# A low-rank adapter kernel: the first sixteen tiles loaded in halves by two DMA queues, and stored four at a time

## The reference

```python
x: (64 sequences, 64 tokens, 1024) f32      ids: (64,) int32, values 3 to 7
A: (8 adapters, 1024, 16) f32               B: (8 adapters, 16, 1024) f32

B_sel, A_sel = B[ids], A[ids]
Bx  = einsum('bni,bri->bnr', x, B_sel)
out = x + einsum('bnr,bor->bno', Bx, A_sel) * 1.0
```

## Time and profile before

| | us |
|---|---|
| median of 3 runs | 92.23 (92.19 to 92.32) |
| the profiled execution | 91.81 |
| its span, first to last instruction | 90.0 |

### The profile page before, as it was taken

One profiled execution on the slowest core, in us unless ns is written; L12 is line 12 of the kernel. 1 busy time (PEld: TensorE's weight loads), 2 busy tenths in 40 slices (PEclk: granted clock), 3 DMA queues, 4 the chain that ended last, 5 costly groups with the idle time before them and its releaser, 6 DMA issues.

```text
span 90.0 us, 3579 instructions
## 1 busy us (share of the span) xinstructions
PE 80.6 (90%) x1451; PEld 60.7 (67%) x1451; DVE 59.7 (66%) x111; ACT 59.4 (66%) x154; POOL 62.9 (70%) x141
## 2 busy tenths in 40 slices
PE   3995999999999999999999999998999999989300
PEld 3974778768787878787777868685778686633100
DVE  0309968277777786859595959595939595999100
ACT  1429869959696969695959686877595868524200
POOL 6103992999999999979696979696859692900000
PEclk9999999999999999999999999999999999999975
DMA  1999999999999999999999999999999999997990
GB/s 29 325 412 422 410 408 408 402 415 413 399 409 404 410 409 400 400 415 413 419 422 413 417 419 410 415 426 406 419 417 415 417 413 400 404 391 306 408 395 36
DMA packets 9249, 34.82 MB, mean 387 GB/s; under 512 B 402, under 2 KB 914, under 8 KB 9234
## 3 DMA queue, kind: packets, MB, share of 16 engines
q1 hardware_dynamic: 7520, 27.79, 77.2%
q10 hardware_dynamic: 1714, 6.82, 18.8%
HBM read 17.83 MB, written 16.78 MB: 384 GB/s over the span
## 4 chain that ended last, share of the span: by engine, by line
PE 83%; DMA 6%; ACT 4%; issue 1%
PE t_bank L255 35%; PE bx_bank L268 21%; PE y_banks L288 18%; DMA x_all<-in_A 6%; PE y_banks L315 2%; PE t_bank L319 2%; ACT x_all L365 1%; PE bx_bank L319 1%; PE y_banks L242 1%; ACT b_table L369 1%; PE bx_bank L315 1%; ACT x_all L424 1%; ACT x_t L377 1%; PE t_bank L315 1%; PE bx_bank L242 0%
## 5 line engine op out<-in xcount | busy, mean ns | idle before, releaser
L465 DVE TENSOR_TENSOR x_all<-y_banks,x_all 128x1024 f32<-128x1024 f32 x29 | 35.5, 1224 | 15.5 <-PE y_banks L288 15.1
L377 ACT COPY x_t<-t_bank 128x512 f32<-128x512 f32 x64 | 34.4, 590 | 13.7 <-PE t_bank L255 12.8
L198 POOL CAST a_duo<-a_table 128x512 fp32r x64 | 36.6, 615 | 3.7 <-PE y_banks L288 2.1
L255 PE MATMUL t_bank<-ident,x_all 128*128 128x128 f32 x256 | 35.0, 280 | 1.2 <-DMA x_all<-in_x 0.8
L255 PEld LDWEIGHTS t_bank<-ident,x_all 128*128 128x128 f32 x256 | 27.4, 141 | 8.4 <-issue 5.2
L188 POOL COPY b_duo<-b_table 128x256 f32 x64 | 22.9, 401 | 5.8 <-PE bx_bank L268 5.8
L268 PE MATMUL bx_bank<-x_t,b_duo 128*32 128x64 f32 x1024 | 20.8, 222 | 0.0
L268 PEld LDWEIGHTS bx_bank<-x_t,b_duo 128*32 128x32 f32 x1024 | 15.7, 109 | 5.5 <-issue 5.5
L288 PE MATMUL y_banks<-a_duo,bx_parts 64*128 64x512 f32 x112 | 17.3, 421 | 0.3 <-issue 0.3
L456 DVE TENSOR_TENSOR bx_parts<-bx_bank,bx_parts 32x64 fp32r<-32x64 f32 x64 | 14.1, 220 | 1.5 <-ACT bx_parts L392 0.4
L392 ACT CAST bx_parts<-bx_bank 32x64 fp32r<-32x64 f32 x64 | 13.0, 204 | 1.9 <-PE bx_bank L268 1.3
(11 more groups left out here) (31 smaller groups left out, 21.2 us busy)
## 6 DMA issues: line engine op xcount, KB each, us to landing
x_all<-in_x SPq DMA_DIRECT2D x3, 3072.0 KB, 30.7
out_y<-x_all ACTq DMA_DIRECT2D x2, 3072.0 KB, 17.8
x_all<-in_x SPq DMA_DIRECT2D x3, 1024.0 KB, 12.4
out_y<-x_all SPq DMA_DIRECT2D x1, 3072.0 KB, 14.5
out_y<-x_all SPq DMA_DIRECT2D x6, 512.0 KB, 4.7
x_all<-in_x SPq DMA_DIRECT2D x4, 512.0 KB, 7.2
x_all<-in_x SPq DMA_DIRECT2D x1, 2048.0 KB, 20.0
out_y<-x_all SPq DMA_DIRECT2D x1, 2048.0 KB, 10.4
```

Of the source, the lines that this page charges most:

```text
L198: last = nc.gpsimd.tensor_copy(a_duo[duo % 2][:, k, :], a_table[:, bass.ds(adapters[k] * BANK, BANK)])
L255: last = nc.tensor.transpose(t_bank[unit % 2][:, c * P:(c + 1) * P], x_all[:, 2 * duo + tile, at:at + P], ident[:, :])
L377: nc.scalar.copy(x_t[duo % 2][:, half * HALF:(half + 1) * HALF, tile, :], t_bank[unit % 2][:, :].rearrange("p (c n) -> p c n", c=HALF)).th ...
L465: nc.vector.tensor_tensor(here, product, here, ALU.add).then_inc(y_drained, 1)
```

## The change

Three things are moved.

Tiles 0 to 15 are now loaded in two halves each. SP's queue takes the even rows (partitions 0, 2, ..., 126) and ACT's queue the odd rows. The semaphore of such a load rises by 32 in all, and the PE waits for 32. The groups are 0, 1, 2 and 3 singly, (4,6), (6,8), (8,12) and (12,16). ACT issues its halves of the first six groups right behind B and the ids, ahead of its first computation; the half of (8,12) in duo 0, and that of (12,16) at the head of duo 2.

Tiles 16 to 31 are loaded by SP whole, as (16,20), (20,24), (24,28) and (28,32). The last two wait for the tables' sources, since they end beyond tile 26.

ACT stores (0,4) at the head of duo 4, (4,8) at the head of duo 7 and (8,12) at the head of duo 10, in place of two stores of six tiles. What SP stores is as before.

```diff
-    LOADS = [(t, t + 1) for t in range(4)] + [(t, t + 2) for t in range(4, 10, 2)]
-    LOADS += [(10, 14)] + [(t, t + 6) for t in range(14, TILES, 6)]
-    STORES_BY_ACT = {6: (0, 6), 9: (6, 12)}
+    LOADS = [(t, t + 1) for t in range(4)] + [(4, 6), (6, 8), (8, 12), (12, 16)]
+    SHARED = len(LOADS)
+    LOADS += [(16, 20), (20, 24), (24, 28), (28, TILES)]
+    SHARED_AT_START = 6
+    SHARED_IN_DUO = {0: 6, 2: 7}
+    STORES_BY_ACT = {4: (0, 4), 7: (4, 8), 10: (8, 12)}
...
-                sp.dma_start(x_all[:, first:end, :], rows[:, first:end, :]).then_inc(x_loaded[n], 16)
+                own = slice(0, P, 2) if n < SHARED else slice(0, P)
+                sp.dma_start(x_all[own, first:end, :], rows[own, first:end, :]).then_inc(x_loaded[n], 16)
...
-                    pe.wait_ge(x_loaded[load], 16)
+                    pe.wait_ge(x_loaded[load], 32 if load < SHARED else 16)
...
+            def load_odd_rows(n):
+                first, end = LOADS[n]
+                own = slice(1, P, 2)
+                act.dma_start(x_all[own, first:end, :], rows[own, first:end, :]).then_inc(x_loaded[n], 16)
+
+            for n in range(SHARED_AT_START):
+                load_odd_rows(n)
...
+                if duo in SHARED_IN_DUO and duo:
+                    load_odd_rows(SHARED_IN_DUO[duo])
                 if duo + 1 < DUOS:
                     copy_x(duo + 1, 0)
                     copy_x(duo + 1, 1)
                 if duo == 0:
                     copy_a(A_BY_ACT[1])
+                    load_odd_rows(SHARED_IN_DUO[duo])
```

## The result

The changed kernel has a median of 92.61 us (91.84 to 94.28, 22 runs) against 92.18 us (91.86 to 92.38, 22 runs) before: a ratio of 1.0041, 95% interval 1.0026 to 1.0056. It is slower by 0.4 us, where 3.2 us were forecast. Six of its 22 executions took 93.2 to 94.3 us, and none of the 22 of before did; the ratio leaves them out, and no trace of one was kept. Its profiled execution took 92.62 us, with a span of 90.6.

A forecast was written before the change was run, and what follows sets the result against it. The prediction took A's load at the start, then unbroken PE work, to bound the kernel, with DMA also near its limit. A's +2.65 and the clock's +0.5 made 3.15 us, so 95.4 us; range 93.3 to 98.2, about 82%.

The forecast's parts named there:

- What bounds the kernel: From 8.81 us the chain is almost unbroken PE work without slack, so delaying A by d delays the end by d.
- A in the shared engines, +2.65: At the start, A's last 1 KB packets alternate with 4 KB packets of x in q10; A lands at 8.7, +2.65 us.
- Rival (c): At the start, engines already hold A's packets when ACT's odd rows arrive; A lands at 6.06, time 92.2; chance 6%.
- ACT's issues, 0: Eight added loads and one store on ACT, 0.4 to 0.5 us each, are covered by A's wait or other waits: 0.
- Tile 0: Its even rows, behind A in q1, come 2.65 us later, at 10.0; one shift with A's, not added.
- Tiles 1 to 15: Their loads carry the same bytes in another order and land before the PE needs them: cost 0.
- loads and stores later on: SP's larger tiles and ACT's earlier stores move no more bytes: cost 0, from -0.1 to +0.3 us.
- The clock, +0.5: The PE waits 3.5 us before tile 0, so its clock may fall: 0 to +1.2 us, taken as +0.5.
- Rival (a), slow halves: Loads of every other row run slower, at three quarters of the rate 98.4 us; chance 12% at 97 to 101.
- The sign: The changed kernel was to be slower by more than 0.2 us, with chance 0.94.

The follow-up runs named there:

- the kernel with q10 full: The kernel before with one more load of 1 MB in 4 KB packets ahead of B on ACT's queue; 94.71 us, ratio 1.0318.
- the stores alone: The kernel before with only ACT's stores changed, to (0,4), (4,8) and (8,12) at the heads of duos 4, 7 and 10; 91.91 us, ratio 0.9982.
- the twelve small DMAs: The kernel before with twelve small DMAs (64 rows of 64 bytes, never read) on ACT's queue behind the ids; 97.46 us, ratio 1.0598.
- whole by SP: The changed kernel's load groups and stores, but SP issues every load whole and ACT none; 91.84 us, ratio 0.9980, and once more 91.93, 0.9996.

## Why the prediction was wrong, point by point

- **What bounds the kernel.** Step failed: "as nothing behind 8.81 has slack, the end by d". The chain of waits showed PE work up to 84.2 us and I read the end off it. The 5 us behind it are the last store, and I did not ask why that took 4.8 us to land, for 1.3 us of bytes (512 KB at 413 GB/s). Where the DMA engines have run dry in part ahead of it, it takes 3.3 to 3.4, as five rows of the table show, though the store before it is still in its queue there. The other 1.5 are backlog, for the most part that of a single DMA engine, and that is the slack. Rows 11 had a share of 0.35 from 86.8 on, and I read only the clock from it. The last store was issued 2.0 us late and landed 0.6 late: this alone takes 1.5 us off.
- **A in the shared engines, +2.65.** Measured 0: A landed at 5.94. The mechanism and its size were right where q10 has work (A landed at 8.12 in the kernel with q10 full, against 8.0 to 8.6 worked out with the same prices). The step that failed is "the first of them at about 1.9 us, well before B is through": I took the issue for the first packet. The trace of before had the row against it, the store issued at 35.56 whose packets began at 39.2, and I read only its issue. Rival (c) had the right outcome for A, with 6%, but gave the start as before.
- **ACT's issues, 0.** Measured +1.3 us at the rounding of A. Two errors: I priced an issue at 0.4 to 0.5 us from a whole load and a store, while these half loads took 0.56 to 0.85 (4.19 us for six), and the ids' issue on ACT already 0.62 in the trace of before; and I let A's lateness cover them. I had written that 0 to 0.5 us would show if A were on time; that was the term to size with care.
- **Tile 0.** Forecast 10.0, as late as A; measured 8.8, late by the odd rows alone (the even rows landed at 6.9). That both shifts are one shift and not added was right.
- **Tiles 1 to 15, loads and stores later on, 0.** Right, by the runs with whole tiles and with the stores alone.
- **The clock, +0.5.** The PE waited 1.39 us ahead of tile 0 and not 3.5, and its transposes there took 272 ns; the term was 0 in the profiled execution. That a long wait costs the clock was borne out by the twelve small DMAs, where it cost about 1.7 us, more than the 1.2 that I had as the most.
- **Rival (a), slow halves.** Fell: 402 to 421 GB/s in the changed kernel from the fourth slice on, with slower stretches at the start (344 GB/s in 6 to 8 us, where the kernel before has 416) for which the PE waited at no later load.
- **The range** went from 93.3 up because all cases but 12% had A late or the halves slow. The sign held, but by a way that I had priced at nothing, so that was luck.

## What to carry to other kernels

Where loads and stores keep the DMA engines full, ask first how long the last store takes to land beyond its own bytes, and whether all DMA engines are busy until then or only one: that backlog is how late the last store may be issued for free, and it caps what an earlier one can gain (whole by SP: issued 0.6 us earlier, landed no earlier). An issue on a computing engine is work of that engine, here 0.6 to 0.7 us for a load of every other row, and what stands behind it in program order is what it costs. And before pricing two transfers against each other, look up in the trace when the second one's packets begin, not when it is issued.

## What the runs showed of the hardware that I had not expected

- A DMA issued on an empty queue while the other keeps the engines busy had its first packet 3.6 to 4.2 us later (35.56 to 39.2, 1.86 to 6.01, 1.22 to 5.09). With the engines idle, SP's first DMA of the program had it 1.1 us behind its issue (0.74 to 1.84) and ACT's 1.6 (0.75 to 2.33).
- An issue on ACT took 0.66 to 0.70 us on the mean, for 4 KB as for 256 KB, and SP's half loads took 0.6 us each with ACT issuing nothing.
- 64-row loads of every other row moved at 402 to 421 GB/s, as full tiles do, once the first of them were through.
- The 16 DMA engines do not end together: in the kernel before one of them works alone on 4 KB packets at the end, 0.16 us each, to 89.17 us, while all were full only to 87.3.
